# Turning stage 2's rows on VectorE with an exchange through DRAM, and moving two of four casts to ScalarE

## The reference

```
h = max(layernorm(x), 0)
msg = relu(h[src] + edge_attr);  agg = zeros.at[dst].add(msg)
a = h + agg
z = a @ W1 + b1                              # 256 -> 512
z = relu((z - mean(z)) / sqrt(var(z) + eps) * gamma + beta)
y = z @ W2 + b2                              # 512 -> 256
... graph norm of y, relu, x = x + h + that
h = max(layernorm(x), 0)
out = x + relu(h @ W + segment_sum((h @ M)[src], dst))
```

## Time and profile before

| | |
|---|---|
| median of 3 runs | 2449.05 us (2446.25 to 2455.07) |
| span of the profiled execution, first to last instruction | 2446.4 us |
| its own time | not recorded apart from its span; the median of the runs lies 2.65 us above the span |
| stage 2 in the trace, first to last matmul of L1268 | 461.8 to about 1615 us |
| PE busy over the span | 96% |
| DVE, ACT, POOL busy over the span | 84%, 70%, 70% |
| TensorE clock over the span | 0.987 of 2.4 GHz |

### The profile page before, as it was taken

How to read it: one execution, slowest core, us unless ns; L and a number is a source line. 1 busy time by engine, 2 the same in 40 slices (tenths; PEclk the granted TensorE clock), 3 DMA queues, 4 the chain that set the end, 5 groups by cost and what they waited for, 6 DMA issues and landing times. The chain is left out here.

```text
span 2446.4 us, 48745 instructions
## 1 busy us (share of the span) xinstructions
PE 2354.5 (96%) x12271; PEld 2013.5 (82%) x12271; DVE 2052.5 (84%) x5707; ACT 1713.3 (70%) x3449; POOL 1708.5 (70%) x1599
## 2 busy tenths in 40 slices
PE   7999998799999999999999999979999999989997
PEld 6888886588888888888888888858989888969996
DVE  8999997598888888888888888967777777749996
ACT  6999997466666666666666666638888888846664
POOL 5777777577767667767766666717777777767774
PEclk8999999899999999999999999999999999999999
DMA  8888995323444444444444344349999999765662
GB/s 257 283 278 275 278 277 170 124 58 127 152 150 158 163 151 147 146 146 166 153 147 145 145 164 154 141 173 405 405 411 413 413 413 413 294 197 162 173 177 88
DMA packets 242978, 531.73 MB, mean 217 GB/s; under 512 B 53856, under 2 KB 141177, under 8 KB 231442
## 3 DMA queue, kind: packets, MB, share of 16 engines
q1 hardware_dynamic: 182434, 459.36, 51.2%
q0 software_dynamic: 59808, 70.24, 10.2%
q10 hardware_dynamic: 592, 0.54, 0.1%
HBM read 340.23 MB, written 286.84 MB: 256 GB/s over the span
## 5 line engine op out<-in xcount | busy, mean ns | idle before, releaser
L1020 POOL DMA_INDIRECT ar<-sum_table,idx x392 | 462.3, 1179 | 177.6 <-issue 96.5
L1067 ACT ACTIVATE r<-pair,bnC,bnA 128x512 f32<-128x512 f32 x392 | 305.9, 781 | 380.2 <-PE pair L1268 377.7
L1471 POOL DMA_INDIRECT x1d_table<-x1r,slot x392 | 383.8, 979 | 139.8 <-issue 123.9
L1175 DVE CAST rH<-r 128x512 fp32r<-128x512 f32 x392 | 391.0, 997 | 97.7 <-ACT r L1067 97.7
L1694 PE MATMUL pair<-Ws,h1T 128*128 128x256 f32 x1568 | 358.7, 382 | 8.9 <-DVE orr L1602 7.4
L1694 PEld LDWEIGHTS pair<-Ws,h1T 128*128 128x128 f32 x1568 | 290.2, 190 | 52.1 <-issue 14.3
L1284 PE MATMUL bank<-rH,W2h 128*128 128x512 f32 (+1 forms) x784 | 305.6, 390 | 1.8 <-ACT yr L1081 1.8
L1284 PE MATMUL bank<-rL,W2h 128*128 128x512 f32 (+1 forms) x784 | 305.7, 390 | 0.0
L1284 PE MATMUL bank<-rH,W2l 128*128 128x512 f32 (+1 forms) x784 | 305.0, 389 | 0.0
L836 PE MATMUL bank<-hr 128*128 128x257 f32 (+1 forms) x1568 | 274.2, 329 | 9.6 <-ACT hr L535 9.6
L1184 DVE TENSOR_TENSOR rL<-r,rH 128x512 fp32r<-128x512 f32 x392 | 271.1, 691 | 13.5
(11 more groups left out here) (239 smaller groups left out, 5234.1 us busy)
## 6 DMA issues: line engine op xcount, KB each, us to landing
xr<-in_x SPq DMA_DIRECT2D x186, 512.0 KB, 3.9
xy_kept<-xy_table SPq DMA_DIRECT2D x57, 1024.0 KB, 20.7
x_table<-x1r SPq DMA_DIRECT2D x97, 512.0 KB, 19.8
out<-orr SPq DMA_DIRECT2D x97, 512.0 KB
xy_table<-xr SPq DMA_DIRECT2D x89, 512.0 KB, 2.6
xy_table<-yr SPq DMA_DIRECT2D x89, 512.0 KB, 3.3
xyr<-xy_table SPq DMA_DIRECT2D x32, 1024.0 KB, 21.0
sum_table<-e_tot SPq DMA_DIRECT2D x99, 128.0 KB, 4.5
```

The lines of the kernel that those rows point to most:

```text
L1020: pool.indirect_dma_start(ar[0:p, s, j, :], None, sum_table[:, :], bass.IndirectOffsetOnAxis(ap=idx[0:p, s, j:j + 1], axis=0), bounds_chec ...
L1067: act.activation(r32[:, m, 0:n], z_ps[m][:, 0:n], ACT.Relu, bias=bnC[:, m:m + 1], scale=bnA[:, m:m + 1]).then_inc(r_kept, 1)
L1175: dve.tensor_copy(rH[:, s, m, 0:n], r32[:, m, 0:n]).then_inc(rh_kept, 1)
L1471: pool.indirect_dma_start(x1d_table[:, :], bass.IndirectOffsetOnAxis(ap=slot[0:p, part, s * T + j:s * T + j + 1], axis=0), x1r[0:p, s, j, ...
```

## The change

Of the 98 groups, PE turns only groups 0, 1 and 97 (`by_tensor`). For the others DVE turns 32x32 blocks of the 128 x 1024 rows in one instruction (`turn_blocks`, L1223), into the tile `W2s`, whose weights have been used by then (`blocks`). SP stores this tile with four DMAs, one for each 32 partitions, to a new DRAM table `ht_table`, in runs of 128 numbers, in such an order that one further DMA, with 4 KB per partition, reads back the fully turned rows (`staged`: `WM`, which replaces `Ws` and `Ms`, for even groups and `W1s` for odd ones). `keep_high` and `keep_low` then read this SBUF tile, in runs of 32 numbers, where they read PSUM before. `add` and `norm` run three groups ahead of the step, not two. The PSUM banks of `hT_ps` become a second buffer of y (`y_ps`). The casts of m = 0 and m = 2 are made by ACT (`HIGH_BY_ACT`), those of m = 1 and m = 3 stay on DVE. POOL reads its indices straight from `ids` (the small copy L1014 goes), and the clearing of `ar` for group k waits for `turn_blocks(k-2)`. The loops of stage 2 are written out in full. `W` and `M` are loaded at the start of stage 3, after its first group loads, and the filler matmuls read `W1s`.

```
+    ht_table = nc.dram_tensor("ht_table", (2, QUADS, SQ, KC, QUADS, P), FP32, kind="Internal").ap()
-        Ws = sb("Ws", [P, KC, CH])
-        Ms = sb("Ms", [P, KC, CH])
+        WM = sb("WM", [P, 2, KC, CH])
+        Ws, Ms = WM[:, 0, :, :], WM[:, 1, :, :]
...
+        def by_tensor(k):
+            return k in (0, 1, NG - 1)
...
+        blocks = W2s[:].rearrange("p a b -> p (a b)")
+        staged = [WM[:].rearrange("p a b c -> p (a b c)"), W1s[:].rearrange("p a b -> p (a b)")]
+        HIGH_BY_ACT = (0, 2)
+        y_ps = [[pair[0][:, c, :] for c in range(KC)], [bank[c][:, :] for c in range(KC)]]
...
+            def turned_part(k, c, n):
+                if by_tensor(k):
+                    return hT_ps[:, c, 0:n]
+                return staged[k % 2][:, c * GC:(c + 1) * GC].rearrange("p (q t n) -> p t q n", q=QUADS, t=T)
...
+                def load_turned(k):
+                    if not exists(k) or by_tensor(k):
+                        return
+                    if k == 3:
+                        sp.wait_ge(q_made, 1)
+                    sp.wait_ge(ht_out[k % 2], 16 * QUADS * exchanges(k))
+                    after(sp, tl_kept, k - 1)
+                    sp.dma_start(staged[k % 2], ht_table[k % 2].rearrange("b p c q n -> (b p) (c q n)")
+                                 ).then_inc(ht_in[k % 2], 16)
...
+                def store_blocks(k):
+                    if not exists(k) or by_tensor(k):
+                        return
+                    sp.wait_ge(blocks_made, blocks_until(k))
+                    after(sp, ht_in[k % 2], 16 * (exchanges(k) - 1))
+                    for q in range(QUADS):
+                        sp.dma_start(ht_table[k % 2, :, :, :, q, :].rearrange("b p c n -> p c b n"),
+                                     blocks[q * SQ:(q + 1) * SQ, :].rearrange("p (c b n) -> p c b n", c=KC, b=QUADS)
+                                     ).then_inc(ht_out[k % 2], 16)
...
+                for k in range(-2, NG + 3):
+                    load_turned(k + 2)
+                    load_rows(k + 5)
+                    store_rows(k + 2)
+                    store_y(k - 2)
+                    clear_slots(k - 1)
+                    store_blocks(k + 3)
...
+                def high(k, m):
+                    if not exists(k) or m not in HIGH_BY_ACT:
+                        return
+                    n = columns(k)
+                    after(act, y_made, k - 1)
+                    act.wait_ge(r_kept, k * HC + m + 1)
+                    act.activation(rH[:, k % 2, m, 0:n], r32[:, m, 0:n], ACT.Copy).then_inc(rh_act, 1)
...
+                def turn_blocks(k):
+                    if not exists(k) or by_tensor(k):
+                        return
+                    dve.wait_ge(h2_done, k + 1)
+                    if k > 2:
+                        dve.wait_ge(ht_out[(k - 1) % 2], 16 * QUADS * exchanges(k - 1))
+                    dve.transpose(blocks.rearrange("p (b t n) -> p t b n", b=KC * QUADS, t=T),
+                                  ar[:, k % AU, :, :].rearrange("p t (b n) -> p t b n", n=SQ)).then_inc(blocks_made, 1)
...
                     for c in range(KC):
-                        last = dve.tensor_tensor(tL[:, s, c, 0:n], hT_ps[:, c, 0:n],
-                                                 tH[:, s, c, 0:n].bitcast(FP32), ALU.subtract)
+                        last = dve.tensor_tensor(nodes_of(tL[:, k % 2, c, 0:n], k), turned_part(k, c, n),
+                                                 nodes_of(tH[:, k % 2, c, 0:n].bitcast(FP32), k), ALU.subtract)
...
+                add(2)
+                turn_blocks(2)
+                for k in range(NG + 2):
+                    step(k)
...
-                act.dma_start(Ws[:], W.rearrange("(k p) n -> p k n", p=P)).then_inc(loaded, 16)
-                act.dma_start(Ms[:], M.rearrange("(k p) n -> p k n", p=P)).then_inc(loaded, 16)
...
+                sp.dma_start(Ws, W.rearrange("(k p) n -> p k n", p=P)).then_inc(w_loaded, 16)
+                sp.dma_start(Ms, M.rearrange("(k p) n -> p k n", p=P)).then_inc(w_loaded, 16)
```

More of the change, by code:

```diff
@@ L927, in gnn_kernel @@
         h2_done = sem("h2_done")
+        blocks_made = sem("blocks_made")
+        ht_out = [sem(f"ht_out{s}") for s in range(2)]
+        ht_in = [sem(f"ht_in{s}") for s in range(2)]
         t2_made = sem("t2_made")
@@ L963, in _, with nodes_of @@
+            def turned_part(k, c, n):
+                if by_tensor(k):
+                    return hT_ps[:, c, 0:n]
+                return staged[k % 2][:, c * GC:(c + 1) * GC].rearrange("p (q t n) -> p t q n", q=QUADS, t=T)
+            def nodes_of(part, k):
+                return part if by_tensor(k) else part.rearrange("p (t q n) -> p t q n", q=QUADS, t=T)
             @block.sync
             def _(sp):
[L966 to L993, removed]
@@ new lines, in clear_slots @@
+                def clear_slots(t):
+                    if not 0 <= t < ET:
+                        return
+                    if t == 0:
+                        sp.wait_ge(blank_made, 1)
+                    sp.dma_start(x1d_table[t * P:(t + 1) * P, :], blank[:]).then_inc(slots_clear, 16)
+                for k in range(3):
+                    load_rows(k)
+                for k in range(-2, NG + 3):
[5 more added lines that the diff above has]
+                    store_blocks(k + 3)
@@ L1113, in _ @@
                 for k in range(2):
-                    for piece in norm((k, k, 0, NU)):
+                    for piece in norm(k):
                         piece()
@@ L1187, in step @@
-                def step(at):
-                    stats(back(at, 2), 0)
-                    keep_low(back(at, -1))
-                    stats(back(at, 2), 1)
-                    high(at, 0)
-                    low(at, 0)
-                    high(at, 1)
-                    low(at, 1)
-                    add(back(at, -2))
-                    high(at, 2)
-                    low(at, 2)
-                    high(at, 3)
-                    low(at, 3)
-                    most(at)
+                    if m in HIGH_BY_ACT:
+                        dve.wait_ge(rh_act, k * len(HIGH_BY_ACT) + HIGH_BY_ACT.index(m) + 1)
+                    else:
+                        dve.wait_ge(rh_kept, k * (HC - len(HIGH_BY_ACT)) +
+                                    sum(1 for i in range(m + 1) if i not in HIGH_BY_ACT))
@@ L1287, in output, with step @@
                         last.then_inc(y_made, 1)
-                def step(at):
-                    turn(back(at, -1))
+                def step(k):
+                    if k + 1 < NG - 1:
+                        turn(k + 1)
                     for m in range(HC):
-                        hidden(at, m)
-                        output(back(at, 1), m)
+                        hidden(k, m)
+                        if m == 0 and k + 1 == NG - 1:
+                            turn(k + 1)
+                        output(k - 1, m)
                 pe.wait_ge(d_made, 1)
@@ L1310, in _ @@
                 last.then_inc(q_made, 1)
-                turn((0, 0, 0, NU))
+                turn(0)
                 pe.wait_ge(var_made, 1)
-                rounds(pe, step, WHOLE - 2, NU, 1, NG - WHOLE + 2 + 1)
+                for k in range(NG + 1):
+                    step(k)
         weights.close()
```

288 lines of the change are left out of this document (164 added, 124 removed).

## The result

| | before | after |
|---|---|---|
| median of 4 runs each, us | 2449.81 (2446.25 to 2455.07) | 2380.72 (2377.86 to 2382.91) |
| span of the profiled execution, us | 2446.4 | 2376.2 |
| TensorE clock over the span | 0.987 | 0.983 |

The ratio of the times is 0.9712, with a 95% interval of 0.9697 to 0.9728: faster by 2.9%, 5.7 us above the 2375 that was forecast. The profiled execution of the changed kernel is the fastest of its four (2377.86 us). All comparisons are of undisturbed executions; one of `e10_casts_dve_tl_early` took 2869.08 us at a granted clock of 0.77 and is left out.

What follows compares the result with a forecast made beforehand. PE was taken as the bound, 11.79 us a group. 93 x (11.79 - 10.98) = 75 us less and 1.3 more gave a span of 2372.4 us; with 2.65 for the median, 2375 us, range 2354 to 2443.

Steps and rivals of the forecast that it cites:

- PE's ceiling: Stage 2 on PE: without its transposes, 0.91 us a group, the pitch goes from 11.79 to 10.88 us.
- Pitch 10.98 through a blocked `tL`: Stage 2 steps: POOL's addition blocks `tL` on DVE, and PE waits 0.1 us a group on average.
- my alternation: POOL's addition falls on `tL` in every second group, otherwise on DVE's addition or transpose; stall up to 0.3 us.
- The transpose at 1.23 us: DVE's block transpose in stage 2 takes as long as its addition over the same 128x1024 numbers, 1.23 us.
- Rival C: Stage 2 on DVE: the block transpose runs at half pace, 2.45 us, 12.35 us a step, 2501 us; chance 0.09.
- DVE's 8.73 us of work: DVE per stage 2 step: 7.50 us plus the transpose make 8.73 of 10.88 us, 2.15 spare.
- Rival B: Stage 2: DVE becomes the bound through POOL's blocking, pitch 11.1 to 11.7 us, 2387 to 2443 us; chance 0.21.
- ACT's casts for nothing: ACT in stage 2 takes two casts of 0.605 us, 8.87 of 10.88 us in all, at no cost.
- DMA share 0.85: Stage 2: the DMA engines' share of busy time rises from 0.41 to near 0.85.
- Rival D: Stage 2: the exchange through DRAM binds; packets at double price need 12.3 us a step, 2496 us; chance 0.11.
- A cover of 4 us on the exchange: Stage 2 stores and load: 13.9 us available, two landings and five issues under 10, so no cost.
- The start of stage 2 "as before": First two or three steps of stage 2: POOL's gathers set the pace as before, so 93 groups count.

Runs made afterwards that it cites:

- `e10_casts_dve_tl_early`: The changed kernel with all four casts on DVE and `tL` made ahead of the cast and remainder of m=1: 2470.04 us, ratio 1.0088.

## Why the prediction was right or wrong

- **PE's ceiling** (0.91 us a group from the transposes): right. Every kernel in which nobody is late comes to 10.88 to 10.91; a quarter is still 2.72.
- **Pitch 10.98 through a blocked `tL`**: right in size and in cause. Measured 10.976; without the addition 10.889; with `tL` early 10.894. I had it blocked in every second group, of 0.1 us on average; it is in 25 of 90, mostly every third group, and each time two steps in a row are longer, mostly by 0.3 to 0.4 us together: 8.5 us in all. By the Trainium skill (SBUF — State Buffer, "SBUF: two separate sides") an instruction of VectorE with two SBUF inputs and one of GpSimd that reads SBUF exclude each other, and the first to start keeps the port pair for its whole length. The new `tL` is blocked as this says (3.94 us for the pair), and so is `rL` (up to 2.67 us for 0.69). Who came first the records cannot settle: in 24 cases of 3.33 to 3.35 us the blocked half of the pair starts 0.36 to 0.38 us before the record of POOL's addition, and yet the last 0.68 us, its own work, lie behind the addition to within 0.12 us. The other half of my alternation (every second group, on DVE's addition or the transpose) is not as put: the addition of POOL fell mostly on the transpose and on the `rL` behind it, seldom on DVE's addition.
- **The transpose at 1.23 us**: 1.246 measured, never more than 1.249 in the middle of stage 2, with POOL's addition beside it or not. Rival C (1.9 us and more) is out.
- **DVE's 8.73 us of work**: 8.63 without POOL's addition. The casts are not the 0.43 us that I named as a sign: 0.622 in the mean, 0.428 at the median for m = 1 and 0.70 for m = 3. POOL's addition is not the cause, since without it the mean is 0.655; the cause is open, and it costs nothing here. The standing still is 1.7 us a group, not 2.4, since part of the addition lies on the transpose. Rival B did not come about, but it stood near: with two casts more, 9.30 us of work, it is what happens, and its condition (every addition blocks in full) then holds by itself.
- **ACT's casts for nothing**: right, 0.633 us against 0.605. Their worth I misjudged, though not in the sum: in the kernel before they bring nothing, here they are what keeps DVE under PE, 84 us by the pitch and 100 by the medians.
- **DMA share 0.85**: 0.75. The engines' time added per group is 0.75 x 10.98 - 4.8 = 3.4 us, not 4.4. The bound from above, 7.5 us, was also worked out wrongly: 0.52 MB at 32.6 us and 1024 packets at twice 0.032 us are 5.2 us of 16 engines, not 6.2, and with the load at most 6.8. Rival D then had 11.6 us a step and not 12.3, under the 11.79 of before; its slower half rested on that error.
- **A cover of 4 us on the exchange**: wrong, though it cost nothing in this kernel. I counted five issues and two landings, under 10 us in all. Left out were the place of the stores on SP's queue, behind a store that waits for POOL (3.7 us from the end of the transpose to the first issue in the group shown, 2.9 at the median), and the issue of the stores, four in 3.1 us at the median and up to 4.0, where two landings of 3.9 left some 2 us for all five issues. The chain is 13.6 us of 14.0 in the group shown, and 12.6 at the median (14.0 less the cover of 1.4).
- **The start of stage 2 "as before"**: the term that was mis-sized, 6.5 us slower over three steps. ACT now makes h of group 2 ahead of z of group 0 and `tH` of group 1, and half of h of group 3 ahead of z of m = 1, and these pieces wait for POOL's first residuals, which stand behind its gathers; the text said that the gathers set the pace "as before" and priced nothing. The forecast was 5.7 us low: 6.5 for this start, 2.0 because 90 steps and not 93 ran at the new pitch, 1.9 because the median stands 4.5 us above the profiled span and not 2.65, and 4.7 the other way in the parts where I had counted 1.3 us more and the table has 3.4 less. Those 3.4 still hold a second thing that I priced at nothing, the end of the stage, where two additions of POOL in a row block one `tL`: 4.4 us by the kernel with `tL` early. That the total came within 6 us is therefore in part luck: terms of 6.5 and 4.4 us are missing, and others make up for a part of them.
- **W and M in stage 3, 1.3 us more**: not seen; stages 3 and 4 together are 1.3 us shorter, within what two executions differ by.

## What to carry to other kernels

When an engine takes over work with room to spare, look for the one instruction with a deadline and put it first in the step: the same 1.7 us of standing still per group cost 7 to 8 us over 90 steps, and 4 more at the end of the stage, where it met `tL`, and next to nothing on `rL` and the casts. Work moved off an engine is worth only what that engine's total, its standing still included, would exceed the bound by: two casts were worth 0 us beside PE's transposes and 84 to 100 us without them. And time an exchange by walking the issuing queue as it stands, with the wait of every entry ahead and the issue time of each DMA; the share of the DMA engines (0.75 here, 0.84 with the stores doubled) says nothing of that chain.

## What the runs showed of the hardware

- A block transpose of VectorE on 128x1024 fp32 numbers takes 1.245 us at the median (1.244 to 1.249 over 89), as the addition of the same count (1.214), and GpSimd's addition beside it (61 of the 89) leaves it alone. A cast from SBUF to SBUF, which has one input too, is blocked (3.20 us for 0.427 in the earlier trace rows; 697 ns in the mean with the addition and four casts on VectorE, 470 without it).
- A store of 128 KB from 32 partitions in runs of 512 bytes took 0.6 to 1.9 us to issue on SP's queue, four in a row 2.6 to 4.0, 3.1 at the median; a load of 512 KB took 0.33.
